# An attention loop on one NeuronCore: values issued for two key steps in every second step

## The chip, the cores and the metric

One Trainium2 chip, one of its NeuronCores. The time is the device time of one launch in microseconds; the kernel before was run three times. The trace is one further execution, taken by the hardware profiler.

## The reference, cut to what matters

The network takes x of shape (8, 256, 32, 32) in float32 and adds four blocks to it, each fed with a group norm of x: a state-space block (L0), an attention (L1), dilated depthwise convolutions with a mix (L2), and an attention between two channel norms (L3). The change is in the attention, which L1 and L3 share. For each sample there are 8 heads of 32 channels and 1024 tokens:

```python
scores = jnp.einsum('bthe,bThe->bhtT', q, k) / jnp.sqrt(jnp.float32(EMB))
attn = jax.nn.softmax(scores, axis=-1)
out = jnp.einsum('bhtT,bThe->bthe', attn, v)
```

## The kernel before, in words

The kernel works sample after sample (8), and in each through the four blocks; `attention(b, a)` runs twice a sample (a = 0 for L1, 1 for L3), 16 times in all. Every engine has one program, written out in order; engines wait for each other by semaphores that count up.

An attention has four phases (`PHASES`): two groups of four heads times two halves of 512 queries. A phase walks over eight key steps (`kt`, 128 keys each; `key_step` numbers them). In a step TensorE (PE) multiplies the transposed scores of the four heads, 98 x 128 by 98 x 512 (L1378), two heads into PSUM banks 2 and 3 and two into banks 4 and 5. Two of the 98 rows carry the negated maximum of each query, as head and rest of a float32r pair. ACT takes the exponential of each pair into the ring `PT`, which has four slots, one for each step (L617). `values(i)` multiplies step i's slot by V into bank 0: four matmuls of 32 columns, one for each head, side by side in the array (L1326). It waits for both exponentials of its step, and at step 0 for the last phase's output to have been read (`o_raw`). The sums over the keys (softmax denominators) come in two ways. For steps 0 to 5 of phases 0 to 2 GpSimd (POOL) adds the slots (L411), in phase 3 DVE does so for steps 0 to 6 (L1004), and `joined_sum` turns these sums into bank 1 by one set of matmuls (L1349). For the other steps `denominators(i)` multiplies the slot by ones into bank 1 (L1337). ACT writes slot i only once the values, and the sum, of step i - 4 are done (L611 to L614).

After its phase's step 0, ACT computes the reciprocal of the denominators of the phase before (L601 logarithm, L605 exponential), and DVE normalizes bank 0 with it (L971, L973).

The maxima come one phase ahead. During phases 0 to 2 PE also computes the next phase's scores with queries on the partitions, in 32 halves of rows, 96 x 128 by 96 x 512 each (L1281, `row_scores`), and DVE takes the maximum of each (L947). How many belong to a step is in `HALF_ROWS = (5, 4, 4, 4, 5, 5, 5, 0)`; `next_rows(most)` issues up to so many of the step's remaining ones. They use the PSUM banks 6 and 7, from the sixth on the banks 1, 7 and 6 in turn, and each waits until the maximum of the last user of its bank is taken (L1280); the sixth also waits for `den_rc`, ACT's reciprocal. In step 7 (`TURN_AT`) `turn_max` transposes the joint maxima of the queries (L954) on PE (L1286), DVE negates them (L961, L963), and two DMAs on SP's queue put them beside the queries (L310); the first scores of the next phase wait for them (`nm_in`, L1372). Two of the rows of step 0 stand ahead of that wait.

PE's order in a step of the kernel before is: scores of a pair, one row half, scores of the other pair, one row half, the values of the step before, its denominators, and the remaining rows (L1364 to L1389). Steps 0 of phases 1 to 3 begin with the last values and denominators of the phase before.

Of the kernel before, what the change touches and what calls it, by code (L numbers as in the profile page):

```python
# [32 lines left out]
KT = L // P  # L33
# [17 lines left out]
PHASES = GROUPS * NC  # L51
HALF_ROWS = (5, 4, 4, 4, 5, 5, 5, 0)
TURN_AT = 7
# [42 lines left out]
def build(nc, x, wpack, vpack, w8, out):  # L96
    with ExitStack() as ctx:
# [981 lines left out]
        def _(pe):  # L1079
# [172 lines left out]
            def attention(b, a, X):  # L1252
# [13 lines left out]
                def row_scores(n, cc):  # L1266

                    ph, j, q = n // PHASE_ROWS, n % PHASE_ROWS // 4, n % 4
                    g, c = divmod(ph, NC)
                    h = GH * g + j  # L1270
                    if c == 0 and q == 0 and cc == 0:
                        pe.wait_ge(*stackedq[g][j](b, (a + 1) * 48))
                        pe.wait_ge(*stackedk[g][j](b, (a + 1) * 48))
                    at = NC * (n % PHASE_ROWS) + cc
                    ahead = 2 * NC if ph == 0 else NC if at < FIRST_ROWS else len(ROW_RING)
                    if ph > 0 and at == FIRST_ROWS:
                        if ph > 1:
                            pe.wait_ge(*den_rc(b, PHASES * a + ph - 1))
                    elif at >= ahead:
                        pe.wait_ge(*r_max(b, halves(a, n, cc) - ahead + 1))  # L1280
                    pe.matmul(PS[:, row_slot(n, cc), :], QS[0:kd, c, h, q * P:q * P + P], KS[0:kd, h, cc * N:cc * N + N],  # L1281
                              start=True, stop=True).then_inc(r_ps.sem, 1)

                def turn_max(ph):
                    pe.wait_ge(*m_both(b, a * PHASES + ph + 1))
                    pe.transpose(PS[0:PHASE_ROWS, 6, 0:P], mboth[:, :], ident[:, :]).then_inc(mt_ps.sem, 1)  # L1286
# [25 lines left out]
                def place(i):  # L1312
                    ph, kt = divmod(i % (PHASES * KT), KT)
                    sums = POOL_SUMS if ph < PHASES - 1 else DVE_SUMS
                    return ph, kt, [k for k in range(KT) if k not in sums]

                def values(i):

                    ph, kt, direct = place(i)
                    g = ph // NC  # L1320
                    pe.wait_ge(*p_sb(b, 2 * i + 2))
                    if kt == 0 and ph > 0:
                        pe.wait_ge(*o_raw(b, i // KT))
                    for j in range(GH):
                        h = GH * g + j
                        ins = pe.matmul(PS[32 * j:32 * j + 32, 0, :], Vt[:, kt, DH * h:DH * h + DH], PT[:, i % PT_RING, j, :],  # L1326
                                        start=(kt == 0), stop=(kt == KT - 1), skip_group_check=True)
                    if kt not in direct:
                        ins.then_inc(pv_ps.sem, 1)

                def denominators(i):

                    ph, kt, direct = place(i)
                    if kt not in direct:
                        return
                    for j in range(GH):
                        ins = pe.matmul(PS[32 * j:32 * j + 32, 1, :], ones32[:, :], PT[:, i % PT_RING, j, :],  # L1337
                                        start=(kt == direct[0]), stop=False, skip_group_check=True)
                    if kt < KT - 1:
                        ins.then_inc(pv_ps.sem, 1)  # L1340

                def joined_sum(ph):

                    if ph < PHASES - 1:
                        pe.wait_ge(*sum_pool(b, pool_sums(a, ph, len(POOL_SUMS) - 1)))
                    else:
                        pe.wait_ge(*sum_dve(b, dve_sums(a, len(DVE_SUMS) - 1)))
                    for j in range(GH):
                        ins = pe.matmul(PS[32 * j:32 * j + 32, 1, :], ones32[:, :], acc[:, ph % 2, j, :],  # L1349
                                        start=False, stop=True, skip_group_check=True)  # L1350
                    ins.then_inc(pv_ps.sem, 1)

                for ph in range(PHASES):
                    g, c = divmod(ph, NC)
                    row = [NC * PHASE_ROWS * (ph + 1), 0]

                    def next_rows(most):
                        for _ in range(min(most, row[1]) if ph < PHASES - 1 else 0):
                            if row[0] % (NC * PHASE_ROWS) == 0:
                                pe.wait_ge(*nm_rest(b, PHASES * a + ph + 1))  # L1360
                            row_scores(*divmod(row[0], NC))
                            row[0], row[1] = row[0] + 1, row[1] - 1

                    for kt in range(KT):  # L1364
                        i = key_step(a, ph, kt)
                        row[1] = HALF_ROWS[kt]
                        if kt == 0:
                            if ph > 0:
                                values(i - 1)
                                denominators(i - 1)  # L1370
                            next_rows(2)
                            pe.wait_ge(*nm_in(b, 32 * (PHASES * a + ph + 1)))  # L1372
                        for pr in range(2):
                            if ph + kt > 0:
                                pe.wait_ge(*p_sb(b, 2 * i - 2 + pr + 1))
                            for jj in range(2):
                                h = GH * g + 2 * pr + jj
                                ins = pe.matmul(PS[:, 2 + 2 * pr + jj, :], KS[:, h, kt * P:kt * P + P], QS[:, c, h, :],  # L1378
                                                start=True, stop=True)
                            ins.then_inc(s_ps.sem, 1)  # L1380
                            next_rows(1)
                        if kt > 0:
                            values(i - 1)
                            if kt == TURN_AT and ph < PHASES - 1:
                                turn_max(ph + 1)
                            denominators(i - 1)
                        elif ph > 0:
                            joined_sum(ph - 1)
                        next_rows(row[1])  # L1389
                values(key_step(a, PHASES - 1, KT - 1))  # L1390
                denominators(key_step(a, PHASES - 1, KT - 1))
                joined_sum(PHASES - 1)
# [37 lines left out]
            for b in range(B):  # L1430
                block0(b)
                group_norm(b, 1)
                attention(b, 0, xg)
                keep_busy(18)
                pe.wait_ge(*o_sb(b, 4))
                project(b, 0, oT)
                group_norm(b, 2)
                block2(b)
                group_norm(b, 3)
                chan_norm(b, 0, xg)  # L1440
                attention(b, 1, xg)
                pe.wait_ge(*o_sb(b, 8))
                chan_norm(b, 1, oT)
                norm_means(b, 4)
                project(b, 1, oT, lambda: norm_variances(b, 4))
                pe.wait_ge(*gn_xa(b, 5))
                pe.wait_ge(*gn_xb(b, 5))
                pe.wait_ge(*x_new(b, 16))
# [15 lines left out]
def key_step(a, ph, kt):  # L1464

    return (PHASES * a + ph) * KT + kt
# [105 lines left out]
```

## Time and profile before

| what | value |
|---|---|
| median of three runs | 5188.22 us (5187.37 to 5195.23) |
| the profiled execution, its own time | 5195.53 us |
| its span, first to last instruction | 5193.8 us |
| mean granted TensorE clock | 0.861 |
| PE busy | 4154.5 us, 80% |
| DVE busy | 3659.1 us, 70% |
| ACT busy | 2120.0 us, 41% |
| POOL busy | 2008.9 us, 39% |

The span is what the profile covers; the execution's own time is 1.7 us longer. Busy shares are means over stages that differ much, so a single stage is read from windows and the timeline. In the timeline the idle time in brackets is that of the engine just before the instruction, with what released it. A group "x8" of the values is four matmuls, recorded in two parts each.

### The profile page before, as it was taken

How to read it: one execution, taken by the hardware profiler on the slowest of the kernel's cores; microseconds unless marked ns; L12 is line 12 of the kernel's file. 1: busy time of each engine (PE TensorE's matmuls, PEld its weight loads, DVE VectorE, ACT ScalarE, POOL GpSimd, SP SyncE). 2: the span in 40 equal slices, each digit the busy share in tenths (PEclk: the TensorE clock that was granted, in tenths of full speed). 3: DMA queues.
4: the chain of work that ended last, by engine and by line, in shares of the span. 5: the costliest groups of instructions: out<-in, count | busy, mean ns of one | idle time of the engine just before them, and what ended most of it. 6: DMA issues, size and time to landing. Idle time of an engine off the chain costs nothing.

```text
span 5193.8 us, 46112 instructions
## 1 busy us (share of the span) xinstructions
PE 4154.5 (80%) x17066; PEld 1944.2 (37%) x17066; DVE 3659.1 (70%) x4992; ACT 2120.0 (41%) x2567; POOL 2008.9 (39%) x681
## 2 busy tenths in 40 slices
PE   5688966889669896698966989668896698966988
PEld 2244422444224442244422444224442244422443
DVE  6865778657776578765787657876578675786756
ACT  4233542335423354243542435424254242542425
POOL 3531535315354153440544505445054450544505
PEclk7789976899769997799977999779997799977989
DMA  1020100211002100022000220002200012000120
GB/s 38 0 58 17 34 9 0 58 22 29 8 0 58 35 15 8 6 53 45 5 8 9 50 49 1 8 9 49 49 1 8 19 40 49 6 3 14 37 49 9
DMA packets 62963, 125.86 MB, mean 24 GB/s; under 512 B 18825, under 2 KB 21001, under 8 KB 62482
## 3 DMA queue, kind: packets, MB, share of 16 engines
q1 hardware_dynamic: 62738, 122.91, 10.2%
q8 instruction: 135, 2.21, 0.2%
q14 instruction: 90, 0.74, 0.0%
HBM read 12.23 MB, written 8.39 MB: 4 GB/s over the span
## 4 chain that ended last, share of the span: by engine, by line
PE 50%; DVE 25%; issue 10%; ACT 6%; SPq 4%; POOL 3%; DMA 3%; DVEq 0%; ACTq 0%; POOLq 0%
PE PS L1378 9%; PE PS L1326 9%; PE PS L1281 9%; PE PS L1114 7%; DVE mx L947 5%; DVE work L839 3%; DVE work L841 3%; PE PS L1173 3%; PE PS L1211 2%; PE PS L1417 2%; PE PS L1089 2%; SPq L293 2%; DMA QS<-nm 2%; SPq L302 2%; POOL work L395 1%
## 5 line engine op out<-in xcount | busy, mean ns | idle before, releaser
L947 DVE TENSOR_REDUCE mx<-PS 128x1 f32<-128x512 f32 x2048 | 1277.9, 683 | 329.5 <-PE PS L1281 328.1
L617 ACT ACTIVATE PT<-PS 128x1024 f32<-128x1024 f32 x1024 | 999.9, 1022 | 813.5 <-PE PS L1378 796.6
L411 POOL TENSOR_TENSOR piece<-PT 128x2048 f32<-128x2048 f32 x48 | 220.3, 4590 | 1954.9 <-ACT PT L617 1954.9
L1281 PE MATMUL PS<-KS,QS 96*128 96x512 f32 x2048 | 848.1, 471 | 132.6 <-DMA KS<-piece 84.4
L411 POOL TENSOR_TENSOR piece<-piece,PT 128x2048 f32<-128x2048 f32 x192 | 879.9, 4583 | 15.5 <-ACT PT L617 0.5
L391 POOL TENSOR_TENSOR work<-work,Crep 128x1024 f32<-128x1024 f32 x256 | 615.8, 2407 | 391.6 <-DVE work L839 192.0
L1378 PE MATMUL PS<-QS,KS 98*128 98x512 f32 x2048 | 670.5, 419 | 37.6 <-DMA QS<-nm 37.4
L1281 PEld LDWEIGHTS PS<-KS,QS 96*128 96x128 f32 x2048 | 379.4, 199 | 619.0 <-DVE mx L947 366.0
L1211 PE MATMUL PS<-dstk,sel 128*128 128x512 f32 (+1 forms) x640 | 317.4, 571 | 321.9 <-DVE work L841 132.3
L1326 PE MATMUL PS<-PT,Vt 128*32 128x512 f32 x4096 | 546.5, 605 | 25.6 <-DVE oT L971 19.3
L545 ACT ACTIVATE PS<-PS,Aneg 128x1024 f32<-128x1024 f32 x256 | 278.3, 1087 | 628.1 <-PE PS L1211 597.4
L1211 PE MATMUL PS<-ustk,sel 128*128 128x512 f32 (+1 forms) x640 | 335.5, 598 | 183.6 <-DVE work L824 86.6
L1378 PEld LDWEIGHTS PS<-QS,KS 98*128 98x128 f32 x2048 | 381.0, 197 | 259.0 <-ACT PT L617 126.3
L1114 PE MATMUL PS<-xg,W 128*128 128x512 f32 x640 | 340.8, 686 | 63.0 <-ACT Brep L473 36.3
L1211 PEld LDWEIGHTS PS<-dstk,sel 128*128 128x128 f32 x640 | 152.7, 268 | 462.9 <-DVE work L839 179.2
L1211 PEld LDWEIGHTS PS<-ustk,sel 128*128 128x128 f32 x640 | 139.3, 256 | 489.5 <-DVE work L824 168.3
L824 DVE TENSOR_TENSOR work<-PS,Brep 128x1024 f32<-128x1024 f32 (+1 forms) x256 | 250.6, 979 | 74.4 <-PE PS L1211 72.2
L1173 PE MATMUL PS<-work,ysel 128*32 128x512 f32 (+1 forms) x1536 | 271.0, 796 | 38.3 <-POOL work L395 30.6
L939 DVE SCALAR_TENSOR_TENSOR piece<-PS,V,piece 128x1024 fp32r<-128x1024 f32 x64 | 82.1, 1283 | 258.2 <-ACT piece L591 258.2
L395 POOL TENSOR_TENSOR work<-work,Crep 128x640 f32<-128x640 f32 x128 | 210.4, 1647 | 138.3 <-DVE work L850 82.6
L376 POOL TENSOR_TENSOR ustk<-work,ustk 64x1024 fp32r<-64x1024 f32 x16 | 37.6, 2349 | 564.4 <-ACT ustk L488 563.8
L1114 PEld LDWEIGHTS PS<-xg,W 128*128 128x128 f32 x640 | 140.3, 224 | 235.8 <-issue 160.3
(203 smaller groups left out, 5209.5 us busy)
## 6 DMA issues: line engine op xcount, KB each, us to landing
QS<-piece SPq DMA_DIRECT2D x384, 128.0 KB, 2.4
KS<-piece SPq DMA_DIRECT2D x384, 128.0 KB, 2.4
xin<-x SPq DMA_DIRECT2D x8, 1024.0 KB
out<-xr SPq DMA_DIRECT2D x8, 1024.0 KB, 4.0
W<-wpack SPq DMA_DIRECT2D x2, 1024.0 KB
QS<-nm SPq DMA_DIRECT2D x128, 8.0 KB, 1.9
W<-wpack SPq DMA_DIRECT2D x1, 576.0 KB
W<-wpack SPq DMA_DIRECT2D x2, 256.0 KB
```

The costliest lines, as they stand in the source:

```text
L391: pool.tensor_tensor(slot, h, Crep[:, at:at + L], ALU.mult).then_inc(hC_sb.sem, 1)
L395: pool.tensor_tensor(two(slot), two(h), Crep[:, None, at:at + W3].broadcast_to((P, 2, W3)), ALU.mult).then_inc(hC_sb.sem, 1)
L411: pool.tensor_tensor(total, first, PT[:, i % PT_RING, :, :], ALU.add).then_inc(sum_pool.sem, 1)
L545: act.activation(dst, src, ACT.Exp, scale=Aneg[:, ps * SG + g:ps * SG + g + 1]).then_inc(dA_sb.sem, 1)
L617: act.activation(PT[:, i % PT_RING, 2 * pr:2 * pr + 2, :], PS[:, 2 + 2 * pr:4 + 2 * pr, :], ACT.Exp, scale=SCALE).then_inc(p_sb.sem, 1)
L947: dve.tensor_reduce(mx[:, at, cc:cc + 1], PS[:, row_slot(n, cc), :], AX.X, ALU.max).then_inc(r_max.sem, 1)
L1114: ins = pe.matmul(PS[:, bank, :], w[:, k, m * P:m * P + P], X[:, k, c * N:c * N + N], start=(k == 0), stop=(k == CT - 1))
L1173: ins = pe.matmul(PS[32 * j:32 * j + 32, c, 0:N if ps < 2 else W3], ysel[:, q % 4, :], src, start=(q % 4 == 0), stop=(q % 4 == 3), skip_gr ...
L1211: ins = pe.matmul(PS[:, slot + c, 0:wc], sel[:, g % 8, :], stk[:, g // 8, at + c * N:at + c * N + wc], start=True, stop=True)
L1281: pe.matmul(PS[:, row_slot(n, cc), :], QS[0:kd, c, h, q * P:q * P + P], KS[0:kd, h, cc * N:cc * N + N], start=True, stop=True).then_inc(r_ ...
L1326: ins = pe.matmul(PS[32 * j:32 * j + 32, 0, :], Vt[:, kt, DH * h:DH * h + DH], PT[:, i % PT_RING, j, :], start=(kt == 0), stop=(kt == KT - ...
L1378: ins = pe.matmul(PS[:, 2 + 2 * pr + jj, :], KS[:, h, kt * P:kt * P + P], QS[:, c, h, :], start=True, stop=True)
```

## The change

In PE's loop over the key steps:

- in steps 2, 4 and 6 the values of the two steps before are issued, with one row half (where one is left) between them; steps 1, 3, 5 and 7 issue none;
- at step 0 of phases 1 to 3 the values of steps 6 and 7 and then the denominators of both are issued, ahead of the first two row halves;
- after the last phase the values of steps 6 and 7 are issued, and the denominators and the joined sum as before;
- `turn_max` in step 7 comes directly after the scores; `joined_sum` at step 0 stays where it was.

```diff
                         if kt == 0:
                             if ph > 0:
+                                values(i - 2)
                                 values(i - 1)
+                                denominators(i - 2)
                                 denominators(i - 1)
                             next_rows(2)
                             pe.wait_ge(*nm_in(b, 32 * (PHASES * a + ph + 1)))
...
-                        if kt > 0:
+                        if kt == TURN_AT and ph < PHASES - 1:
+                            turn_max(ph + 1)
+                        if kt > 0 and kt % 2 == 0:
+                            values(i - 2)
+                            next_rows(1)
                             values(i - 1)
-                            if kt == TURN_AT and ph < PHASES - 1:
-                                turn_max(ph + 1)
-                            denominators(i - 1)
-                        elif ph > 0:
+                        elif kt == 0 and ph > 0:
                             joined_sum(ph - 1)
                         next_rows(row[1])
+                values(key_step(a, PHASES - 1, KT - 2))
                 values(key_step(a, PHASES - 1, KT - 1))
                 denominators(key_step(a, PHASES - 1, KT - 1))
                 joined_sum(PHASES - 1)
```

## Rows read from the trace of the kernel before

**Rows 1.** The page: busy time by engine, and the chain that ended last.

```profile
PE 4154.5 (80%) x17066; PEld 1944.2 (37%) x17066; DVE 3659.1 (70%) x4992; ACT 2120.0 (41%) x2567; POOL 2008.9 (39%) x681
...
PE 50%; DVE 25%; issue 10%; ACT 6%; SPq 4%; POOL 3%; DMA 3%; DVEq 0%; ACTq 0%; POOLq 0%
```

**Rows 2.** Windows, phases 1 to 3: stretch, length, busy PE PEld DVE ACT POOL (count), clock, DMA share.

```profile
1222.00:1250.00 28.00, 27.49 (x151) 12.77 (x151) 21.53 (x37) 16.74 (x18) 22.53 (x6) 1.00 0.01 1
1250.00:1279.00 29.00, 28.10 (x154) 12.92 (x153) 21.98 (x37) 16.72 (x18) 23.19 (x6) 1.00 0.01 1
1279.00:1304.00 25.00, 20.83 (x121) 6.80 (x121) 16.20 (x11) 17.67 (x20) 0.89 (x1) 1.00 0.00 1
```

**Rows 3.** Timeline of ACT, the once-a-phase logarithm: start, us, engine, line, op [idle before].

```profile
1281.53 0.60 ACT L601 ACTIVATE PS<-PS 128x512 f32<-128x512 f32 x1
1301.42 0.58 ACT L601 ACTIVATE PS<-PS 128x512 f32<-128x512 f32 x1 [2.90 <-PE PS L1349]
...
4923.56 0.60 ACT L601 ACTIVATE PS<-PS 128x512 f32<-128x512 f32 x1
4943.47 0.58 ACT L601 ACTIVATE PS<-PS 128x512 f32<-128x512 f32 x1 [2.90 <-PE PS L1349]
```

**Rows 4.** Timeline, phase 2 of an attention, step 2 into step 3.

```profile
1259.69 0.73 PE L1281 MATMUL PS<-KS,QS 96*128 96x512 f32 x2
...
1260.27 0.63 PE L1378 MATMUL PS<-QS,KS 98*128 98x512 f32 x2
...
1261.43 0.40 PE L1281 MATMUL PS<-KS,QS 96*128 96x512 f32 x1
...
1261.77 1.07 PE L1326 MATMUL PS<-PT,Vt 128*32 128x512 f32 x8
```

**Rows 5.** Timeline, the same phase, step 4 into step 5.

```profile
1265.83 0.96 PE L1281 MATMUL PS<-KS,QS 96*128 96x512 f32 x3
1266.36 3.08 DVE L947 TENSOR_REDUCE mx<-PS 128x1 f32<-128x512 f32 x5 [0.58 <-PE PS L1281]
...
1267.11 0.50 PE L1281 MATMUL PS<-KS,QS 96*128 96x512 f32 x1
```

**Rows 6.** Timeline, the same phase, its first scores, and step 1.

```profile
1250.27 0.64 PE L1378 MATMUL PS<-QS,KS 98*128 98x512 f32 x2
...
1254.50 0.50 PE L1281 MATMUL PS<-KS,QS 96*128 96x512 f32 x1 [0.43 <-ACT lr L605]
...
1255.61 1.28 DVE L947 TENSOR_REDUCE mx<-PS 128x1 f32<-128x512 f32 x2
```

**Rows 7.** Timeline, the same phase, step 7 and the entry to phase 3.

```profile
1275.10 0.19 DVE L954 TENSOR_REDUCE mboth<-mx 128x16 f32<-128x32 f32 x1
...
1275.45 0.28 PE L1286 MATMUL PS<-ident,mboth 128*16 128x128 f32 x1
...
1276.54 1.04 PE L1326 MATMUL PS<-PT,Vt 128*32 128x512 f32 x8
...
1277.40 1.04 PE L1337 MATMUL PS<-PT,ones 128*32 128x512 f32 x8
...
1278.84 1.21 PE L1378 MATMUL PS<-QS,KS 98*128 98x512 f32 x4 [0.40 <-DMA QS<-nm]
```

**Rows 8.** Timeline, phase 3.

```profile
1283.63 1.07 PE L1326 MATMUL PS<-PT,Vt 128*32 128x512 f32 x8 [1.21 <-DVE oT L971]
...
1285.45 1.94 ACT L617 ACTIVATE PT<-PS 128x1024 f32<-128x1024 f32 x2 [0.85 <-PE PS L1378]
...
1288.10 1.07 PE L1326 MATMUL PS<-PT,Vt 128*32 128x512 f32 x8
...
1289.10 1.21 PE L1378 MATMUL PS<-QS,KS 98*128 98x512 f32 x4
...
1289.95 1.94 ACT L617 ACTIVATE PT<-PS 128x1024 f32<-128x1024 f32 x2 [0.43 <-PE PS L1378]
...
1298.57 1.07 PE L1326 MATMUL PS<-PT,Vt 128*32 128x512 f32 x8 [0.39 <-ACT PT L617]
```

## The prediction, made before the changed kernel was run

> **What bounds the kernel now.** I read the page first. TensorE is busy for 80% of the span, and of the chain that ended last it holds 50%, DVE 25% and ACT 6% [rows 1]. The change touches one loop only, so I read phases 1, 2 and 3 of one attention by windows: PE fills 27.49 of 28.00 and 28.10 of 29.00 us in the first two, and 20.83 of 25.00 in the last. DVE has 22 us of work in each of the first two, and the granted clock is 1.00 [rows 2]. So PE's own order of work sets phases 0 to 2. Third, the once-a-phase logarithm of the ACT shows how regular this is: the last two of the third and fourth phase lie 19.89 us apart in sample 1 and 19.91 us in sample 7 [rows 3]. A change per attention can therefore be multiplied by 16 (8 samples, 2 attentions). Last I read the timeline at single instructions. I call S the scores of one pair of heads (two matmuls), r a row half of the next phase's scores (one matmul, whose maximum DVE takes), V the values of one key step, D a denominator, E an exponential pair on ACT.
>
> **Prices.** In a step of four rows S S r S S take 1.16 us (1260.27 to 1261.43), so r and S matmuls stand 0.235 us apart, up to 0.29 behind a V; V starts 0.34 us after the last r (0.10 more than an r would) [rows 4], and the next full-width matmul 1.00 us after V (1288.10 to 1289.10) [rows 8]. Where V is followed by D it takes 0.86 us (1276.54 to 1277.40) [rows 7]. So one run of narrow matmuls costs about 0.23 us more than its V's. An r occupies its PSUM slot for long: DVE starts 0.54 us after an r that follows V (0.44 otherwise), takes 3.08/5 = 0.62 us, and the third r after it starts about 0.2 us behind DVE's end: the r listed at 1267.11 with 0.50 us instead of 0.40 is already held so [rows 5]. There are three slots.
>
> **The change part by part.**
> (a) V leaves steps 1, 3, 5 and 7; steps 2, 4 and 6 carry two, steps 0 of the next phase carry V6 and V7. Work on PE is the same. In phases 0 to 2 the order of the even steps is V r V r, so the two V's do not adjoin; there narrow runs go from nine to eight in a phase (V0 to V5, V6, D6-V7-D7 and the joined sum, against three times two, V6-V7-D6-D7 and the joined sum). That is worth 0.23 us, and is inside what follows.
> (b) The odd steps lose their 1 us of V, and this was the time in which DVE caught up. I lay the order out again by these prices, in us from the phase's first S (1250.27 in phase 2 [rows 6]).
> Step 1: the fifth row half waits for the ACT's reciprocal at +4.23 as before, and DVE is in its normalization until +5.34 [rows 6]. Its maximum is done at 5.96. The order r S r r r now reaches the row that needs this slot at 5.5, and it has to wait until 6.16. S of step 2 then starts at 6.40 (without V0 ahead of it), the two V's follow, and step 3 begins at 10.47; before it began at 1260.27, that is +10.00, for phase 2's first S stood at 1250.27, ten microseconds ahead [rows 4, 6]. Loss 0.46. In phase 0 there is no normalization and the same sum gives -0.06.
> Steps 3 and 4: waits of 0.09 and 0.10 us (a slot; E of step 3 for the second S), +0.04 in all.
> Steps 5 and 6: five rows each. Without V between them step 5's last three rows and step 6's first two must go at DVE's pace: with maxima ending at 18.80, 19.42, 20.04, 20.66 the rows start at 18.38, 19.00, 19.62, 20.24, 20.86 where PE alone would send most 0.235 apart. Step 5 to step 7 takes 7.30 us; before it was two steps of 3.41 (nine wide matmuls and V with its gaps, and 0.1 of slot wait), 6.81. Loss 0.49.
> (c) Step 7: before, V6 stood between the last S and the transpose (turn) of the maxima, and turn followed at 1275.45, by the prices 2.01 us after the step's first S (four S matmuls and V6), with DVE's joint maximum just done at 1275.29 [rows 7]. Now turn comes right behind S. The last two rows, behind a V, start 0.48 and 0.24 us before S(7); DVE needs 0.54 from the first of them, 2 x 0.62, 0.19 for the joint maximum and some 0.13 around it, so turn starts 1.62 us after step 7's first S, where PE is ready after 0.94: a wait of 0.68. Then V6, V7, D6, D7 in one run and two rows, 0.21 + 0.88 + 2 x 0.86 + 0.97 + 0.57 = 4.35 us, against 3.49 before (0.21 + 0.88 = 1.09 is turn to V7, 0.86 V7 to D7, 0.97 is from D7 to the idle of 0.40 ahead of S [rows 7]). From S(7) to the next phase's S it is 1.62 + 4.35 = 5.97 us, before 2.01 + 3.49, rounded 5.49: loss 0.48 in phases 0 and 1. At the entry to phase 3 the S waited for the DMA of the maxima, 3.39 us after turn [rows 7]; that wait is now covered, the run ends later instead, 1.62 + 3.78 - 0.03 = 5.37 against 2.01 + 3.39 = 5.40: -0.03. The maxima's DMA so costs nothing more, and SP has nothing else queued behind it. POOL's sums (22 to 23 of 28 us [rows 2]) start from E of step 1, which comes no later than before, and a longer phase gives them more room.
> (d) Phase 3, no rows. Before, V0 waited for the normalization for 1.21 us and held S of step 2 behind it, so that ACT idled 0.85 us ahead of 1285.45 [rows 8]. Moved to step 2, V0 holds nothing, and E(1), which ends at 1285.45 - 0.85 = 1284.60, is followed at once: a gain. But two V's in a row now keep S(3), S(5), S(7) from ACT, which has only one step of scores ahead. From E's end to V 0.71 us (1287.39 to 1288.10), two V's 0.86 + 1.00, S to E 0.85 (1289.10 to 1289.95), E pair 1.94: 5.36 us for two steps. Before, two steps took 4.50 (1285.45 to 1289.95) [rows 8]. E(7) ends at 1284.60 + 3 x 5.36 = 1300.68, V7 follows at 1300.73; before at 1298.57. Loss 2.16 with the gain counted.
> Sum of an attention: phase 0 -0.06+0.04+0.49+0.48 = 0.95; phase 1 0.46+0.04+0.49+0.48 = 1.47; phase 2 0.46+0.04+0.49-0.03 = 0.96; phase 3 2.16; together 5.54. Times 16: 88.6 us. On the profiled execution's 5195.53 that is 5284.1, on the median of the three runs, 7.3 lower, 5276.8.
> Bounds: in phases 0 to 2 each of the waits can't be under 0 (then -0.23 remains of a phase) nor over a whole V moved, 1 us, at each of steps 1, 5 and 7. I take the values laid out, since they use the rows' own pitches.
>
> PE's order matters in (c) and (d): the 1.21 us of PE idle at V0, with S ready behind it, shows it holding to program order [rows 8]. The Trainium skill says the same (TensorE: Matmul & The Clock Gate, section "Step-by-step: what each phase is for"): weight loads may be pulled ahead, matmuls stay in program order; if S could pass V, (d) would be a gain.
>
> **Rivals.**
> 1. Faster: the narrow runs are what counts. Six fewer in an attention (one in each of phases 0 to 2; in phase 3 the V's do adjoin, three fewer), if DVE's slack (6 of 28 us in a phase [rows 2]) and ACT's hide every wait: 96 x 0.23 = 22 us, time 5166. It decides if rows wait for nothing and ACT keeps 2.25 us a step in phase 3. For it: DVE and ACT aren't full on average. Against it: the slot wait already seen, and 1.86 us of V behind which ACT has nothing. Beside it, the Trainium skill (TensorEngine Tiling (Array Packing), "Key Properties") says that a change of tiling mode drains the engine; the trace's price for it is the 0.23 us above, and by that rule alone the result would be this rival's. Chance 0.05.
> 2. Slower only in phase 3: the slots have more slack than I laid out and turn's wait is short. 16 x 2.16 less 48 x 0.23: +24, time 5212. Chance 0.12.
> 3. Slower by more: DVE's backlog doesn't drain in the even steps, steps 1 and 3 pay too and turn waits a further 0.6. About 0.8 more in each of 48 phases: +127, time 5315. For it: DVE busy 22 of 28 us in phase 2. Against: in an even step of 4 us it has 2.5 us of work. Chance 0.12.
> 4. PE's waits in phase 3 (the longest I lay out is 1.5 us) let the granted clock fall to 1.2 GHz, so two V's take 1.9 us longer in about two double steps: +60 more, time 5338. Against it: at the 1.21 us wait and in the last window at 83% busy it stayed at 1.00 [rows 2, 8]. Chance 0.03.
> The change does less than its name in phases 0 to 2 (a row lies between the V's); that is in all cases.
>
> **How the numbers follow.** My own case has 0.68: 5277. The range of 5236 to 5320 leaves out rivals 1, 2 and 4, 0.20 together, and takes in rival 3 and errors of half of the 3.4 us that phases 0 to 2 lose. Under 0.2% (10 us) can't be told from no change. Faster 0.05 is rival 1 nearly whole; same 0.02 is a mixture of rivals 1 and 2; slower 0.93 the rest.
>
> **What would show it.** In the changed kernel's timeline: the logarithms of phases 2 and 3 some 22 us apart instead of 19.89; ACT idle of about 1.4 us ahead of E in steps 3, 5, 7 of phase 3 and none in the even ones; a PE wait of 0.5 to 0.8 us for DVE at the transpose; row maxima back to back across steps 5 and 6, with waits of row matmuls for DVE larger than before; phase 1 some 30.2 us instead of 28.7. I am wrong if the phases 0 to 2 keep 28.7 us, or if S passes the V's in phase 3, or if the clock in the attention falls below 1.00.

## The result, and the profile after

The changed kernel takes 5321.31 us (median of 4 runs, 5318.31 to 5323.82), the kernel before 5190.31 us beside it (4 runs): a ratio of 1.0251, 95% interval 1.0233 to 1.0269. It is 131 us slower. I had forecast 5277, +89, with a range up to 5320.

The page after, the same two lines as [rows 1]:

```profile
PE 4215.4 (79%) x17066; PEld 1959.5 (37%) x17066; DVE 3668.4 (69%) x4992; ACT 2119.8 (40%) x2567; POOL 2007.5 (38%) x681
...
PE 47%; DVE 28%; issue 10%; ACT 7%; SPq 3%; POOL 2%; DMA 2%; DVEq 0%; ACTq 0%; POOLq 0%
```

The instructions are the same in number. PE's share of the chain falls from 50 to 47%, DVE's and ACT's rise from 25 to 28 and from 6 to 7%: PE now waits for them. The page's PE busy rose by 61 us with no work added; part of that is work at half clock, as will be seen.

Where the time is, I read from the timelines of all 16 attentions: from the first scores of a phase to those of the next (in phase 3 to the last group of the joined sum), means in us:

| phase | before | after | more | forecast |
|---|---|---|---|---|
| 0 | 29.06 | 30.02 | 0.96 | 0.95 |
| 1 | 28.83 | 30.75 | 1.92 | 1.47 |
| 2 | 28.75 | 30.20 | 1.45 | 0.96 |
| 3 | 21.48 | 25.15 | 3.67 | 2.16 |
| sum | 108.12 | 116.12 | 8.00 | 5.54 |

8.00 x 16 = 128.0 us; the spans of the two profiled executions differ by 5317.4 - 5193.8 = 123.6. (The first experiment's expectation has 21.51 and 3.64 for phase 3, read 0.03 too long.) From the first scores of a step to those of the next, phase 1 lost 0.73 us in steps 1 and 2 (forecast 0.46), 0.25 in steps 3 and 4 (0.04), 0.51 in steps 5 and 6 (0.49) and 0.41 in step 7 (0.48).

Windows of phases 1 to 3 of the attention shown before (columns as in [rows 2]; phase 1's first scores are now at 1243.84):

```profile
1244.00:1274.00 30.00, 28.42 (x153) 12.61 (x151) 21.98 (x37) 16.75 (x18) 22.90 (x5) 1.00 0.01 1
1274.00:1304.00 30.00, 28.45 (x153) 13.27 (x153) 22.17 (x37) 16.74 (x18) 22.72 (x5) 1.00 0.00 1
1304.00:1332.00 28.00, 22.98 (x128) 7.51 (x120) 14.93 (x8) 17.42 (x20) 0.19 (x1) 0.94 0.00 1
```

The last window has a granted clock of 0.94. In [rows 2] it was 1.00. The logarithms of [rows 3] are now 23.68 us apart, 3.79 more than 19.89:

```profile
1307.31 0.60 ACT L601 ACTIVATE PS<-PS 128x512 f32<-128x512 f32 x1
1330.99 0.58 ACT L601 ACTIVATE PS<-PS 128x512 f32<-128x512 f32 x1 [2.90 <-PE PS L1349]
```

The timeline of phase 3 after, what answers to [rows 8]:

```profile
1308.44 3.84 ACT L617 ACTIVATE PT<-PS 128x1024 f32<-128x1024 f32 x4
...
1309.51 0.73 PE L1380 MATMUL PS<-QS,KS 98*128 98x512 f32 x2 [1.30 <-ACT PT L617]
1310.43 0.76 PE L1380 MATMUL PS<-QS,KS 98*128 98x512 f32 x2 [0.18 <-ACT PT L617]
...
1311.12 3.53 PE L1326 MATMUL PS<-PT,Vt 128*32 128x512 f32 x16
...
1314.59 1.20 PE L1380 MATMUL PS<-QS,KS 98*128 98x512 f32 x4
1315.41 3.87 ACT L617 ACTIVATE PT<-PS 128x1024 f32<-128x1024 f32 x4 [3.13 <-PE PS L1380]
...
1318.07 1.92 PE L1326 MATMUL PS<-PT,Vt 128*32 128x512 f32 x16
...
1320.79 3.87 ACT L617 ACTIVATE PT<-PS 128x1024 f32<-128x1024 f32 x4 [1.50 <-PE PS L1380]
```

E(1) and E(2) follow each other in one block (3.84 us at 1308.44): V0 no longer holds the scores of step 2, as forecast. Then ACT stands: 1.50 us ahead of 1320.79, where I had 1.48. Two steps take 1320.79 - 1315.41 = 5.38 us, forecast 5.36. But the first pair of values takes 3.47 us (1311.12 to 1314.59), the others 1.85. The granted clock in its stretch, with the one behind it:

```profile
1309.50:1311.00 1.50, 1.30 (x4) 0.60 (x4) 0.81 (x2) 1.50 (x2) 0.00 (x0) 1.00 0.00 0
1311.00:1312.50 1.50, 1.50 (x9) 0.40 (x12) 1.50 (x1) 1.28 (x2) 0.00 (x0) 0.50 0.06 11
1312.50:1314.50 2.00, 2.00 (x12) 0.20 (x4) 1.97 (x2) 0.00 (x0) 0.00 (x0) 0.52 0.00 0
1314.50:1317.00 2.50, 1.79 (x10) 0.97 (x6) 0.60 (x1) 1.59 (x2) 0.00 (x0) 1.00 0.00 0
```

0.50 is the lower level, 1.2 GHz. Here the fall came behind waits of 1.30 and 0.18 us; before, there was the one of 1.21 us [rows 8], and the scores behind V0 waited for nothing. In the trace before, the granted clock is 1.00 throughout phase 3 in all 16 attentions; in the trace after, it falls once in each. In 14 it falls 0.2 to 2.0 us after the end of the wait of 1.30 us, in six of these ahead of the one of 0.18. In the other two (first scores of phase 3 at 3053.8 and 4600.1) it stays at 1.00 through the first pair of values and falls ahead of the second, behind waits of 0.70 and 0.18 us. The longest group of values in phase 3 takes 2.66 to 3.53 us, where 1.92 is usual.

In phase 1 (first scores at 1243.84), the places that answer to [rows 4 to 7]:

```profile
1248.07 0.50 PE L1281 MATMUL PS<-KS,QS 96*128 96x512 f32 x1 [0.42 <-ACT lr L605]
...
1250.01 0.47 PE L1281 MATMUL PS<-KS,QS 96*128 96x512 f32 x1 [0.49 <-DVE mx L947]
1250.32 0.62 PE L1380 MATMUL PS<-QS,KS 98*128 98x512 f32 x2
...
1251.81 1.07 PE L1326 MATMUL PS<-PT,Vt 128*32 128x512 f32 x8
1252.81 0.50 PE L1281 MATMUL PS<-KS,QS 96*128 96x512 f32 x1
1253.24 1.07 PE L1326 MATMUL PS<-PT,Vt 128*32 128x512 f32 x8
1254.23 0.50 PE L1281 MATMUL PS<-KS,QS 96*128 96x512 f32 x1
1254.57 0.64 PE L1380 MATMUL PS<-QS,KS 98*128 98x512 f32 x2
...
1262.36 1.84 PE L1281 MATMUL PS<-KS,QS 96*128 96x512 f32 x4
1264.04 0.63 PE L1380 MATMUL PS<-QS,KS 98*128 98x512 f32 x2
...
1270.06 0.28 PE L1286 MATMUL PS<-ident,mboth 128*16 128x128 f32 x1 [0.44 <-DVE mboth L954]
```

and DVE beside the last of them:

```profile
1261.16 5.47 DVE L947 TENSOR_REDUCE mx<-PS 128x1 f32<-128x512 f32 x9 [0.73 <-PE PS L1281]
```

At +6.17 the row waits for its slot (forecast 6.16). The lone rows between values cost more than I took: V to V is 1253.24 - 1251.81 = 1.43 us and V to S over one row 1.33, where my prices gave 1.33 and 1.23. In step 5 four rows take 1.68 us until S, nearly twice their pitch, and DVE takes nine maxima back to back. At the transpose PE waits.

### The profile page after: what moved, and what is told of

Its sections match the earlier page's. It is cut to its first block, busy times and chain, and to the rows that moved or that the text cites. A ratio compares the mean times of both kernels' runs of the same rounds, so it can differ in the third digit from the quotient of the medians.

```text
span 5317.4 us, 46112 instructions
## 1 busy us (share of the span) xinstructions
PE 4215.4 (79%) x17066; PEld 1959.5 (37%) x17066; DVE 3668.4 (69%) x4992; ACT 2119.8 (40%) x2567; POOL 2007.5 (38%) x681
## 4 chain that ended last, share of the span: by engine, by line
PE 47%; DVE 28%; issue 10%; ACT 7%; SPq 3%; POOL 2%; DMA 2%; DVEq 0%; ACTq 0%; POOLq 0%
PE PS L1326 9%; DVE mx L947 9%; PE PS L1281 7%; PE PS L1114 7%; PE PS L1380 6%; DVE work L839 3%; ACT PT L617 3%; DVE work L841 3%; PE PS L1173 3%; PE PS L1211 3%; PE PS L1421 2%; PE PS L1089 2%; SPq L293 2%; PE PS L1337 2%; POOL work L395 1%
## 5 line engine op out<-in xcount | busy, mean ns | idle before, releaser
L1281 PE MATMUL PS<-KS,QS 96*128 96x512 f32 x2048 | 879.4, 475 | 153.9 <-DMA KS<-piece 84.6
L1380 PE MATMUL PS<-QS,KS 98*128 98x512 f32 x2048 | 681.8, 424 | 78.1 <-ACT PT L617 52.6
L1281 PEld LDWEIGHTS PS<-KS,QS 96*128 96x128 f32 x2048 | 393.2, 199 | 691.4 <-DVE mx L947 428.6
## 6 DMA issues: line engine op xcount, KB each, us to landing
QS<-piece SPq DMA_DIRECT2D x384, 128.0 KB, 2.4
KS<-piece SPq DMA_DIRECT2D x384, 128.0 KB, 2.4
```

## The experiments

All times are medians of 4 to 10 launches beside the kernel before on the same chip (its medians there: 5187.85 to 5194.08 us); differences are to the changed kernel's 5321 unless it says otherwise. The ratio to the kernel before, with its 95% interval, stands in brackets; where it overlaps the changed kernel's 1.0233 to 1.0269, the total alone doesn't show a gain, and the phases have to. Phase times are means over 16 attentions, as in the table, from one trace of each kernel.

**Phase 3 in the old order.**

```diff
-                        if kt > 0 and kt % 2 == 0:
+                        if ph == PHASES - 1 and kt > 0:
+                            values(i - 1)
+                        elif kt > 0 and kt % 2 == 0:
...
-                values(key_step(a, PHASES - 1, KT - 2))
```

> The changed kernel, but phase 3 issues the values in the old order, one key step in each step. Summed over the 16 attentions, the two traces put phase 3 at 21.51 us before and 25.15 after. Theory (pairs of V starve ACT in phase 3, and the clock falls there): phase 3 is back near 21.5 us, 16 x 3.64 = 58 us less than 5321, so about 5263. Rival (phase 3 is longer because of what phase 2 hands over, its four narrow groups at the phase's entry): phase 3 keeps over 24 us and the time stays above 5300.

Measured 5268.30 us (ratio to before 1.0147, 1.0132 to 1.0162): 53 less. Phase 3 is 21.48 us, phases 0 to 2 stay at 30.14, 30.79 and 30.24. The theory holds; phase 3's own order makes its 3.67 us.

**PE kept at work in phase 3's first wait.**

```diff
+                        if ph == PHASES - 1 and kt == 1:
+                            for _ in range(5):
+                                pe.matmul(PS[:, 7, 0:P], mean128[:, :], mean128[:, :], start=True, stop=True)
```

> The changed kernel with five unneeded 128x128 float32 matmuls into the unused bank 7 behind the scores of step 1 of phase 3, where PE waits for ACT. Theory (the wait of PE lets the granted clock fall to 1.2 GHz, so V0 and V1 take 3.47 us instead of 1.86): clock 1.00 through phase 3, V0-V1 at 1.86 us, 16 x 1.6 = 26 us less, about 5296. Rival (the V pair is slow for another reason, the DVE's sum and the write of the ring that run beside it): V0-V1 stays at 3.5 us and the time at 5321 or a little over.

Measured 5307.07 us (1.0221, 1.0204 to 1.0238): 14 less. Its timeline of phase 3, from the same attention:

```profile
1307.22 1.28 PE L1388 MATMUL PS<-mean 128*128 128x128 f32 x10
...
1308.69 0.73 PE L1380 MATMUL PS<-QS,KS 98*128 98x512 f32 x2 [0.19 <-ACT PT L617]
1309.60 0.73 PE L1380 MATMUL PS<-QS,KS 98*128 98x512 f32 x2 [0.18 <-ACT PT L617]
...
1310.27 1.92 PE L1326 MATMUL PS<-PT,Vt 128*32 128x512 f32 x16
...
1312.12 1.21 PE L1380 MATMUL PS<-QS,KS 98*128 98x512 f32 x4
```

The scores start as soon as ACT allows, the first pair takes 1.85 us as all others, and in none of the 16 attentions does a pair take over 1.93. DVE's sum ran beside it just as before, so the rival is out. Phase 3 is 23.62 us in the mean, 2.14 over the kernel before: the forecast's 2.16 was the starving alone, and the clock is the other 1.53. That would be 24 us; the total gave 14, since phase 2 took 0.31 us more in the mean and the stretch between the two attentions of a sample 1.3 us more. The traces show what most of this is. The longer phase 2 ends in a wait of PE for the DMA of the maxima, and in the same 4 us (1300 to 1304) one packet of queue q8, whose kind is "instruction", is moved (packets, MB, share):

```profile
1303.81 1.20 PE L1380 MATMUL PS<-QS,KS 98*128 98x512 f32 x4 [1.10 <-DMA QS<-nm]
...
q8 instruction: 1, 0.02, 2.2%
```

With the filler such a packet meets this DMA at the entry to phase 3 in 8 of 16 attentions, in the changed kernel in 5, and PE's waits there add up to 6.05 us against 2.02, which is 0.25 of the 0.31. The stretch between the attentions spends 15.8 us at 1.2 GHz in the mean with the filler, 13.2 without; half of the difference is the 1.3 us. In these two traces about 10 of the 24 us that the fallen clock costs in phase 3 thus come back behind it.

**The two values adjoining.** The row between them is left to the rows behind.

```diff
                             values(i - 2)
-                            next_rows(1)
                             values(i - 1)
```

> The changed kernel without the row half between the two values of steps 2, 4 and 6, so that they adjoin. Theory A (each change of the matmul's width costs, as the lone row between two V's shows: V r V r S takes 0.99 + 0.43 + 0.99 + 0.34 against 0.86 + 0.99 + 0.28 x 2): 0.34 us less in each of 144 pairs, 49 us less if nothing else waits; I expect about half of it, 5295, because the rows now come together and wait for DVE. Rival (DVE sets the pace of phases 0 to 2 now, so PE's savings are lost): 5321 within 5 us.

Measured 5313.72 us (1.0231, 1.0216 to 1.0247): 8 less, under a third of what I expected and near the rival; the interval overlaps the changed kernel's. Phases 1 and 2 shrink by 0.27 and 0.20 us, not by three times 0.34. Phase 1 wins 0.34 in steps 1 and 2 and 0.16 in steps 3 and 4, but nothing in 5 and 6 (step 5 takes 3.21 us instead of 2.85), and it gives back 0.17 in step 7: at the transpose PE now waits longer for the DVE.

```profile
1267.57 0.28 PE L1286 MATMUL PS<-ident,mboth 128*16 128x128 f32 x1 [0.82 <-DVE mboth L954]
```

That is 0.82 against 0.44. A PE saving ahead of a DVE bound is mostly lost. Phase 3, which this edit leaves alone, is 24.81 us, 0.34 shorter: the clock fell in 12 attentions only. The sixth experiment comes back to this.

**Values of step 6 ahead of the transpose.**

```diff
                         if kt == TURN_AT and ph < PHASES - 1:
+                            values(i - 1)
                             turn_max(ph + 1)
...
-                                values(i - 2)
                                 values(i - 1)
```

> The changed kernel, but the values of step 6 are issued in step 7 ahead of the transpose of the maxima in phases 0 to 2, as before the change. Theory (PE stands 0.6 us at the transpose for DVE's joint maximum): the wait goes, one more narrow run costs 0.23, so 0.4 us less in each of 32 phases 0 and 1 and nothing in phase 2, 13 us less, about 5308. Rival (the wait is only moved, DVE is late all the same): 5321 or up to 11 slower by the added run.

Measured 5327.65 us (1.0265, 1.0238 to 1.0291), the profiled execution 5315.77; the runs lie 30 us apart, so the total says only that nothing large was gained. The phases do not move (30.16, 30.81, 30.19). The wait at the transpose is gone, and a new one is there:

```profile
1269.29 0.28 PE L1286 MATMUL PS<-ident,mboth 128*16 128x128 f32 x1
1270.02 1.06 PE L1326 MATMUL PS<-PT,Vt 128*32 128x512 f32 x8 [0.45 <-ACT PT L617]
```

V7 waits for step 7's exponentials. My theory of the transpose was wrong in this: its wait hid inside another that ends later.

**Step 7 as before the change.** The last experiment plus the denominators of step 6 behind the transpose.

```diff
                             turn_max(ph + 1)
+                            denominators(i - 1)
...
-                                denominators(i - 2)
```

> The changed kernel with step 7 of phases 0 to 2 as before the change: values of step 6, transpose, denominators of step 6, and values and denominators of step 7 at the next phase's step 0. With the values of step 6 alone moved ahead of the transpose, the trace showed no wait at the transpose but one of 0.45 us of V7 for the exponentials of step 7. Theory (D6 behind V7 leaves nothing that PE can do until step 7's exponentials are done; the transpose's wait hid in the same time): with D6 between, both waits are gone, first scores of step 7 to those of the next phase take 5.5 us instead of 6.0, 0.5 x 32 = 17 us less, about 5304. Rival (the end of a phase is set by DVE or the maxima's DMA): 6.0 us stays, 5321 to 5328.

Measured 5303.39 us (1.0221, 1.0206 to 1.0236): 18 less, expected 17. Phases 0 and 1 are 0.38 and 0.47 shorter. The work that the old order had between V6 and V7 was what covered ACT.

**Fewer rows in the steps without values.**

```diff
-HALF_ROWS = (5, 4, 4, 4, 5, 5, 5, 0)
+HALF_ROWS = (5, 3, 6, 3, 6, 3, 6, 0)
```

> The changed kernel with the row halves dealt out as 5, 3, 6, 3, 6, 3, 6, 0 over the steps instead of 5, 4, 4, 4, 5, 5, 5, 0: fewer in the steps without values. Theory (in a step without values the rows outrun the DVE, and PE waits for a slot: 0.5 us in step 1, together 0.9 us about step 5): these waits go, about 0.6 us in phase 0 and 1.1 in phases 1 and 2, 16 x 2.8 = 45 us less, 5276. Rival (DVE's maxima are the bound in any order, or the six rows of the even steps wait as long as the others did): 5321 within 8.

Measured 5314.56 us (1.0242, 1.0227 to 1.0257): 7 less, where I expected 45, and the interval overlaps the changed kernel's. Step 5 did lose its wait (first scores of step 5 to those of step 6: 2.02 us, from 2.85), but step 6 took 4.84 instead of 4.49, and phase 0, which had little to win, got 0.50 longer. Phases 0 to 2 take 90.99 us together, as they did (90.97): the waits moved with the rows. The 7 us come from phase 3, 24.69 us instead of 25.15, which the edit leaves alone. Its waits are the same, but the clock fell in 11 of 16 attentions. In this one it stayed, and the first pair takes 1.85 us (the last line is a window over phase 3, its clock 1.00):

```profile
419.93 0.73 PE L1380 MATMUL PS<-QS,KS 98*128 98x512 f32 x2 [1.30 <-ACT PT L617]
420.85 0.73 PE L1380 MATMUL PS<-QS,KS 98*128 98x512 f32 x2 [0.18 <-ACT PT L617]
421.51 1.92 PE L1326 MATMUL PS<-PT,Vt 128*32 128x512 f32 x16
423.36 1.19 PE L1380 MATMUL PS<-QS,KS 98*128 98x512 f32 x4
...
415.00:441.00 26.00, 22.06 (x136) 8.70 (x133) 14.93 (x9) 17.61 (x20) 0.00 (x0) 1.00 0.00 1
```

The third to sixth experiments all leave phase 3 alone, and it is 0.16 to 0.46 us shorter in them, with the clock falling in 12, 13, 12 and 11 attentions: 3 to 7 us of each total that the edit didn't make.

**Halved maxima, on both kernels.**

```diff
-dve.tensor_reduce(mx[:, at, cc:cc + 1], PS[:, row_slot(n, cc), :], AX.X,
+dve.tensor_reduce(mx[:, at, cc:cc + 1], PS[:, row_slot(n, cc), 0:N // 2], AX.X,
```

> The changed kernel with DVE's maxima taken over the first 256 of each row half's 512 columns only; the softmax is then scaled by another number, which it divides out. Every maximum should take some 0.35 us instead of 0.62. To be read beside the kernel before with the same edit, since the part ahead of phase 0 is paced by DVE in both and gets shorter by several us an attention in both. Theory (the row matmuls that outrun DVE in steps 1 and 5, and the late joint maximum at the transpose, are what phases 0 to 2 lose): phase 1 goes from 30.75 to about 29.3, phases 0 and 2 by 0.9 and 1.2, and the difference between the two kernels falls from 131 to about 85 us. Rival (the order itself costs, narrow and wide matmuls in turn and V7 behind step 7's exponentials): phase 1 stays over 30.3 and the difference over 115.

> The kernel before with the same halved maxima. Theory: phases 0 to 2 lose only the 0.1 us of slot wait in each step of five rows, phase 1 from 28.8 to 28.4 to 28.6, and the part ahead of phase 0 gets 5 to 7 us shorter in each attention: about 5090. Rival (maxima bound phases 0 to 2 here too): phase 1 under 28.

Measured 5218.44 us for the changed order (1.0055, 1.0039 to 1.0071) and 5110.40 us for the order before (0.9849, 0.9833 to 0.9864): the difference is 108 us instead of 131. Phase 1 is 29.77 against 28.29. Of the 1.92 us that it lost, 0.44 goes with the DVE; of phase 2's 1.45, 0.52; phase 0's loss is 1.10 instead of 0.96. In phases 0 to 2 together that is 0.82 of 4.33 us, 13 us of the kernel. Phase 3 gives 16 more, because its clock fell in 6 attentions only; why it fell less often is not shown, and the stretches outside the phases take some of the 29 back. So the DVE's pace is real but a fifth of what phases 0 to 2 lose, and behind it stands a second bound. The new waits of the changed order with halved maxima, in steps 4 and 7 of phase 1:

```profile
1231.83 0.68 PE L1380 MATMUL PS<-QS,KS 98*128 98x512 f32 x2
...
1232.69 0.30 PEld L1380 LDWEIGHTS PS<-QS,KS 98*128 98x128 f32 x2 [0.38 <-ACT PT L617]
...
1246.23 1.06 PE L1326 MATMUL PS<-PT,Vt 128*32 128x512 f32 x8 [0.47 <-ACT PT L617]
```

A step of four rows without values takes PE 1.9 us. ACT needs 1.94 for its exponentials and DVE 4 x 0.62 = 2.5 for its maxima. Take one away, and the other holds PE. Phase 3 of the changed order is 24.14 us with halved maxima, and its longest pair of values is over 2 us in those 6 attentions only.

**A lag of two steps without pairs, on the kernel before.** Phase 3 alone; the second has the five filler matmuls in step 1.

```diff
-                        if kt > 0:
+                        if ph == PHASES - 1 and kt > 0:
+                            if kt > 1:
+                                values(i - 2)
+                        elif kt > 0:
                             values(i - 1)
...
+                values(key_step(a, PHASES - 1, KT - 2))
                 values(key_step(a, PHASES - 1, KT - 1))
```

> The kernel before, but in phase 3 each step issues the values of two steps before (none in step 1, one key step in each of 2 to 7, the last two at the end). Theory (only the pair starves ACT; the lag itself takes V0's wait for the normalization off the scores of step 2): E of step 2 comes 0.85 us earlier and the pace stays 2.25 us a step, phase 3 is 0.85 us shorter, 13.6 us less than 5189, about 5176, if the clock stays at 1.00. If PE's waits in steps 1 and 2 let the clock fall as in the changed kernel: V0 and perhaps V1 at half clock, 1 to 2 us more, 5190 to 5205. Rival (the lag itself costs, not the pair): phase 3 over 24 us, 5250.

> The same with the five unneeded 128x128 matmuls in step 1 of phase 3. Theory: clock 1.00 throughout, 5176. Rival (the clock does not depend on them, or they hold the scores of step 2 up): as without them, or up to 5 us more.

Measured 5205.54 us (1.0029, 1.0018 to 1.0039) and 5200.93 us (1.0016, 1.0006 to 1.0027), both slower than before. Without filler the logarithms of phases 2 and 3 are 19.47 or 19.48 us apart in 4 attentions and 20.64 to 21.02 in 12, with it 19.46 or 19.47 in all 16, against 19.89 in the kernel before. Two of them, without filler where the clock stayed, and with filler:

```profile
1279.76 0.60 ACT L601 ACTIVATE PS<-PS 128x512 f32<-128x512 f32 x1
1299.23 0.58 ACT L601 ACTIVATE PS<-PS 128x512 f32<-128x512 f32 x1 [2.90 <-PE PS L1349]
...
1289.32 0.61 ACT L601 ACTIVATE PS<-PS 128x512 f32<-128x512 f32 x1
1308.78 0.58 ACT L601 ACTIVATE PS<-PS 128x512 f32<-128x512 f32 x1 [2.90 <-PE PS L1349]
```

So the lag is not what costs: its phase is 0.42 us shorter if the clock holds (I expected 0.85; E(3) then waited 0.64 us for its scores instead of 0.19 and took half back), and the pair is. But the total of the second is 13 us over before, not 7 under. Its phase 2 took 29.07 us instead of 28.75 and the stretch between the attentions 115.4 instead of 114.4. Most of the first is again the DMA of the maxima: a packet of the instruction queue met it at the entry to phase 3 in 8 attentions instead of 3, and PE's waits there add up to 13.9 us instead of 9.6, 4.2 of phase 2's 5.1. Of the second, the 17.4 us at 1.2 GHz instead of 16.7 explain about a third; the rest stays open.

**The best arrangement of pairs that the runs pointed to.**

```diff
+                        if ph == PHASES - 1 and kt > 0:
+                            values(i - 1)
+                        elif kt > 0 and kt % 2 == 0:
+                            next_rows(1)
                             values(i - 2)
-                            next_rows(1)
                             values(i - 1)
```

together with step 7 as before the change.

> The arrangement of pairs that the runs so far point to: in phases 0 to 2 the two values adjoin with the spare row half ahead of them instead of between, step 7 as before the change, and phase 3 with values in each step as before. From the changed kernel's 5321: 53 us less for phase 3 (measured), 18 for step 7 (measured), 8 to 12 for the adjoining values (measured with the rows behind them; ahead of them DVE has three rows to work on during the pair), about 5238. It stays slower than the 5188 of before if DVE's pace in the steps without values is what is left; rival (width changes are what is left): under 5188.

Measured 5222.16 us (1.0062, 1.0044 to 1.0080): 99 less than the changed kernel, 16 better than expected, and still slower than before. Phases 1 and 2 are 29.65 and 29.61 us. No version that was run beats the kernel before, the halved maxima aside.

## Why the prediction was wrong

The direction and the mechanisms (b) and (d) were right, (c) was right in size but not in its place, the sum was two thirds of what was measured, and the time lies 1.3 us above the range. The forecast missed by 44 us. The phases hold 39 of them: 24 in phase 3, which is the clock, and 15 in phases 0 to 2 (4.33 us lost where I had 3.38).

- **Rival 4, the clock: this is the step that failed.** I gave it 0.03, because the clock had stayed at 1.00 at a wait of 1.21 us, and set my sum without it. The changed order has a wait of 1.30 us and one of 0.18 behind it, and the clock fell in every attention of its trace, which I had named as a sign of being wrong. Sized by the filler: 25.15 - 23.62 = 1.53 us of a phase, 24 us in phase 3 and 14 in the total. Had I taken it as part of the forecast, I would have been at 5291 to 5301. Rival 4's own 60 us was too much: it had two slow double steps in each phase 3, the trace has one slow pair. One wait that did no harm was also weak evidence: in the last experiment, with phase 3 in the old order, the clock fell in one attention right behind the same 1.21 us.
- **(d), the starving of ACT in phase 3**, forecast 2.16, measured 2.14 with the clock held. Period 5.38 against 5.36, E(2) behind E(1) at once. This part was right in mechanism and size.
- **(b), prices of lone rows.** I used the price of an entry and an exit from rows in which several wide matmuls stood between. With one between, V to V is 1.43 us instead of 1.33, and the same 0.1 again behind V1 in step 2. Phase 1's first scores of step 3 came at +10.73, I had 10.47; of step 5 at 17.35, I had 16.88; of step 7 at 24.69, I had 24.18. From 0.26 in the first pair the gap grew to 0.51, and to 0.56 at the phase's end. This is the second term that was too small: steps 1 to 4 of phase 1 lost 0.98 us where I had 0.50.
- **(b), the slot waits** came where I put them, at +6.17 and in step 5, where nine maxima stand back to back.
- **(b), what the waits are worth.** I took them as the cause of the loss. They are its first layer: with the maxima halved, 1.48 of phase 1's 1.92 us and 0.93 of phase 2's 1.45 remain, in ACT's pace in the steps without values, in V7's wait and in the lone rows. By steps, 0.47 of phase 1's remainder is in steps 1 and 2, 0.24 in steps 3 and 4, 0.33 in steps 5 and 6, and 0.42 in step 7, where V7 waits; how ACT's pace and the lone rows share the first three was not split further.
- **(c), the transpose.** The wait for DVE came (0.44 of idle PE), and the phase's end lost 0.52 where I had 0.48. But I named the transpose as its place, and moving V6 in front of it changed nothing. The late one is V7 behind E(7), because D6 had gone behind it. One reading was off: from D7 to the idle of 0.40 us [rows 7] it is 1.04 us (1277.40 to 1278.44), not 0.97. It stands on both sides of the sum for phases 0 and 1; at the entry to phase 3 the scores came 3.92 us after the transpose, where I had 3.75.
- **Phase 0** came at 0.96, forecast 0.95, but by luck. Its start runs at 1.2 GHz for a time that differs between attentions, and the kernel before had more of it (5.2 us in the mean against 4.6). In the three attentions where both had 3.7 to 3.9 us of it, phase 0 lost 1.39 to 1.50.
- **Rival 1** (widths alone) is refuted by the order with halved maxima and by the adjoining pairs: 8 us for 144 narrow runs less. The Trainium skill's rule (TensorEngine Tiling (Array Packing), "Key Properties"), that a change of mode drains the engine, agrees with the 0.1 us on either side of a run; it decides nothing where another engine is late.
- **Rivals 2 and 3** are out: phases 0 to 2 lost 69 us of 131, and the waits in steps 1 and 3 are those laid out. Rival 3's time, 5315, is nearer than mine, but its further waits did not come; the clock and the lone rows filled their place.

## What to carry to other kernels

Work that is spread through a loop on the busy engine also gives its partners time. Before gathering it, compare the shortest new step with what each partner must do in one step (here 1.9 us against 1.94 and 2.5), and the longest with how far the partners can run ahead (here one step of scores). When a wait is found, look for the one that ends just behind it before counting it as a gain. And a wait that is new on TensorE should be priced at both levels of its clock, also when a wait of nearly the same length did no harm in the old order. A difference of a few us in the total is no finding before the traces show that it lies in the stretch that the edit touched.

## What the runs showed of the hardware

**The clock and small waits.** Counted over phase 3 of all 16 attentions in the traces of 13 kernels: behind a wait of 1.30 us, in most cases with one of 0.18 us after 0.7 us of scores, the granted clock fell from 1.00 to 0.50 in 16 of 16 attentions of the changed kernel, and in 12, 13, 12, 11 and 6 of 16 in five others whose phase 3 has the same instructions. With single values behind such a wait it fell in 12 of 16. Behind the wait of 1.21 us of the old order it fell in 1 of 64. With 1.28 us of filler matmuls in the wait it fell in none of 32. The waits alone thus don't decide it.

**What a fallen clock costs.** 1.53 us of a phase 3 of 25.15, but 14 us of the total and not 24. In the ten kernels with whole maxima other than the lag with filler, the stretch from one attention of a sample to the next takes 112.5 to 114.4 us, with 13.2 to 16.7 us at 1.2 GHz; less half of that time it is 105.5 to 106.1 us in every one. Its length thus goes with its time at the lower clock, and that was shortest, 13.2 us, in the kernel in which the clock fell in every phase 3.

**Small DMAs and the instruction queue.** The two DMAs of the maxima were followed through 624 entries to phases 1 to 3. The later of them to land took 1.86 to 1.91 us where no packet of the instruction queue started beside them (481 entries), and 1.86 to 3.67 us, median 2.88, where one did (143). A small edit to PE's program changed which entries it met: at phase 3, 3 or 5 of 16 without the filler, 8 of 16 with it.
